# Decoder, one core: the heads' copy of causal attention placed ahead of the exponentials, its residual added by VectorE, and the opening loads split over three queues

## The reference, cut to what matters

```
L0: x1 = ln(x  + recurrence(x))                 # gates from block-diagonal w_in, w_a (8 blocks of 32x32)
    x2 = ln(x1 + retention(x1, ctx))            # position rotation and decay from tables
    x3 = ln(x2 + mixture_of_experts(x2))        # 8 experts, 2 per token
L1: x4 = ln(x3 + causal_attention(x3))          # the block that most of the change touches
    x5 = ln(x4 + cross_attention(x4, ctx))      # 16 heads
    x6 = ln(x5 + hashed_ffn(x5))
```

```
q, k, v = x3 @ wq, x3 @ wk, x3 @ wv             # per head
q, k    = rope(first half of the features), rest as it is
p       = softmax(q k^T / 128 - 1e30 * (i < j)) # i query, j key
out     = sum over heads of (p v) @ wo
x4      = ln(x3 + out)
```

## Time and profile before

| | us |
|---|---|
| median of three runs | 1661.8 (1661.14 to 1669.12) |
| the profiled execution, its own time | 1667.65 |
| its span, first to last instruction | 1665.9 |
| busy in the span: TensorE, VectorE, ScalarE, GpSimd | 1527.8, 1140.6, 801.7, 578.7 |
| mean granted clock of TensorE, as a share of full speed | 0.977 |

### The profile page before, as it was taken

How to read it: one execution, slowest core, us unless ns; L and a number is a source line. 1 busy time by engine, 2 the same in 40 slices (tenths; PEclk the granted TensorE clock), 3 DMA queues, 4 the chain that set the end, 5 groups by cost and what they waited for, 6 DMA issues and landing times.

```text
span 1665.9 us, 34482 instructions
## 1 busy us (share of the span) xinstructions
PE 1527.8 (92%) x12806; PEld 1364.2 (82%) x12806; DVE 1140.6 (68%) x2334; ACT 801.7 (48%) x1527; POOL 578.7 (35%) x679
## 2 busy tenths in 40 slices
PE   3888898899999999788888699999989999999997
PEld 2677777799999999777777578888879999999997
DVE  3899987756655565146777358877867768676775
ACT  5777742244544455236666444545434444443443
POOL 2666651212112120047776211212104444343444
PEclk8999999899999999999999899999999999999999
DMA  5122253212323330152233132121134553635443
GB/s 188 64 77 76 70 189 115 83 39 89 96 95 101 101 102 26 49 200 74 77 91 96 65 124 77 53 78 53 53 73 93 104 121 83 123 85 110 97 92 72
DMA packets 118829, 152.03 MB, mean 91 GB/s; under 512 B 10330, under 2 KB 103716, under 8 KB 118180
## 3 DMA queue, kind: packets, MB, share of 16 engines
q1 hardware_dynamic: 111540, 129.75, 28.4%
q0 software_dynamic: 6144, 16.79, 3.6%
q10 hardware_dynamic: 1008, 3.67, 0.6%
HBM read 111.37 MB, written 38.80 MB: 90 GB/s over the span
## 4 chain that ended last, share of the span: by engine, by line
PE 29%; DVE 11%; issue 7%; DMA 5%; ACT 4%; SPq 1%; POOL 1%; DVEq 0%; ACTq 0%; POOLq 0%
PE psum L518 7%; PE psum L1788 4%; DMA arena_x<-wT_d 3%; PE psum L1772 3%; PE psum L485 3%; PE psum L493 2%; PE psum L1766 2%; DVE psum L2358 2%; PE psum L1749 2%; PE psum L1488 1%; ACT arena_y L1519 1%; DMA wT_d<-arena_w 1%; DVE C_st L437 1%; PE psum L477 1%; PE psum L1485 1%
## 5 line engine op out<-in xcount | busy, mean ns | idle before, releaser
L2129 POOL TENSOR_TENSOR d_g_parts<-arena_w,d_g_parts 128x512 fp32r<-128x512 f32 x128 | 167.8, 1311 | 248.6 <-ACT d_g_parts L2261 240.9
L518 PE MATMUL psum<-d_v_high,d_g_parts 128*128 128x256 f32 x1024 | 205.1, 284 | 4.0 <-POOL d_g_parts L2129 2.3
L518 PE MATMUL psum<-d_x_parts,d_v_high 128*128 128x256 f32 x1024 | 193.5, 287 | 1.7 <-DVE d_x_parts L513 1.7
L518 PE MATMUL psum<-m_w_high,m_h_parts 128*128 128x256 f32 x1024 | 188.0, 285 | 0.0
L1192 ACT ACTIVATE arena_x<-psum,b_e 128x512 f32<-128x512 f32 x128 | 88.2, 689 | 190.1 <-PE psum L518 90.7
L518 PEld LDWEIGHTS psum<-d_v_high,d_g_parts 128*128 128x128 f32 x1024 | 167.5, 190 | 6.5 <-POOL d_g_parts L2129 4.1
L1120 POOL DMA_INDIRECT arena_x<-x_d,slot_row x64 | 66.9, 1045 | 293.6 <-PE psum L1166 229.3
L518 PEld LDWEIGHTS psum<-d_x_parts,d_v_high 128*128 128x128 f32 x1024 | 159.0, 191 | 8.6 <-DVE arena_w L2364 4.1
L518 PE MATMUL psum<-m_xF_parts,m_w_high 128*128 128x512 f32 x512 | 160.2, 395 | 2.1 <-DVE m_xF_parts L513 2.1
L518 PEld LDWEIGHTS psum<-m_w_high,m_h_parts 128*128 128x128 f32 x1024 | 160.9, 192 | 0.0
L2261 ACT ACTIVATE d_g_parts<-arena_w 128x512 fp32r<-128x512 f32 x128 | 80.8, 631 | 153.3 <-DVE arena_w L2364 152.4
(11 more groups left out here) (279 smaller groups left out, 3694.0 us busy)
## 6 DMA issues: line engine op xcount, KB each, us to landing
arena_x<-wT_d SPq DMA_DIRECT2D x128, 256.0 KB, 6.4
arena_y<-in_L_ffn_w SPq DMA_DIRECT2D x16, 1024.0 KB, 7.9
x_d<-arena_x SPq DMA_DIRECT2D x32, 256.0 KB, 2.2
y_d<-arena_x SPq DMA_DIRECT2D x16, 512.0 KB, 9.0
arena_x<-kv_d SPq DMA_DIRECT2D x16, 512.0 KB, 3.3
kv_d<-arena_x SPq DMA_DIRECT2D x9, 512.0 KB, 3.0
arena_x<-in_x SPq DMA_DIRECT2D x16, 256.0 KB, 2.9
arena_x<-in_ctx SPq DMA_DIRECT2D x16, 256.0 KB, 3.2
```

The costliest lines, as they stand in the source:

```text
L518: ins = nc.tensor.matmul(dst, left[a_], right[b_], start=start and k == 0, stop=stop and k == 2, skip_group_check=True)
L2129: nc.gpsimd.tensor_tensor(K["gP"][:, s % 4, 1], K["g"][:, s % 2], K["gP"][:, s % 4, 0].bitcast(F32), ALU.subtract).then_inc(d_gl, 1)
```

## The change

Three edits.

**1. The opening.** The first load on SP is only the identity part of the constants, then comes x of unit 0, then the six vectors and the mask. These (but for x, which has its own semaphore) count on `s_const`: N_EARLY is 8 in place of 28. Of the 16 gate blocks every second one is issued by SP and every other by ScalarE, on a semaphore of their own, `s_diag`. GpSimd issues the rest of the constants (`s_tables`) and the four weights (`s_weights`). TensorE waits for `s_diag` ahead of the first gate products and for `s_weights` in pass 4. VectorE's three instructions that read tables go into a function `setup_tables`, run in pass 2 behind a wait for the tables; GpSimd waits for the tables in its pass 2. ScalarE waits for five counts of `s_setup` in place of ten.

**2. Causal attention, residual.** The identity products are gone; the two products with `wo` start the bank. VectorE adds x3 to bank 7 into a new SBUF tile `r4` (semaphore `c_r4`), and statistics and x4 are made from `r4`. TensorE's wait for bank 7 is now for `c_r4`, and so is ScalarE's wait ahead of x3 (which four units share) and the wait in the cross attention stage.

**3. Causal attention, order.** On ScalarE the heads' copy stands ahead of the exponentials.

```diff
-        loads = [(const[:, :], a["constants"])]
+        loads, tables_in, weights_in = [], [(const[:, P:], a["constants"][:, P:])], []
...
-        N_EARLY = len(loads) + len(diag)
+        N_EARLY = 1 + len(loads)
...
         def setup_sync(sp):
+            sp.dma_start(const[:, 0:P], a["constants"][:, 0:P]).then_inc(s_const, 16)
+            sp.dma_start(A["x"][:, 0], x_u[0]).then_inc(a_in[0], 16)
             for dst, src in loads:
                 sp.dma_start(dst, src).then_inc(s_const, 16)
             sp.wait_ge(s_zero, 1)
-            for dst, src in diag:
-                sp.dma_start(dst, src).then_inc(s_const, 16)
+            for dst, src in diag[::2]:
+                sp.dma_start(dst, src).then_inc(s_diag, 16)
...
+            for dst, src in tables_in:
+                pool.dma_start(dst, src).then_inc(s_tables, 16)
+            for dst, src in weights_in:
+                pool.dma_start(dst, src).then_inc(s_weights, 16)

         def setup_scalar(act):
-
+            act.wait_ge(s_zero, 1)
+            for dst, src in diag[1::2]:
+                act.dma_start(dst, src).then_inc(s_diag, 16)
...
+        def setup_tables(dve):
+            dve.wait_ge(s_tables, 16)
+            ...                                  # even_heads, odd_heads, causal
+        N_DECAY = 5
...
+                    if t.fixed and t.n == 1:     # TensorE, ahead of the gate products
+                        pe.wait_ge(s_diag, 16 * len(diag))
...
+                if t.fixed and t.n == 2:         # VectorE
+                    setup_tables(dve)
...
                 if u3:
-                    done(pe, c_x4, u3.back(1))
+                    done(pe, c_r4, u3.back(1))
                     done(pe, c_os, u3)
                     for b in range(UB):
-                        nc.tensor.matmul(bank(7)[:, b * D:(b + 1) * D], ident, C["x3"][:, u3.c % 4, b, :],
-                                         start=True, stop=False)
                         for h in range(H1):
                             ins = nc.tensor.matmul(bank(7)[:, b * D:(b + 1) * D], C["oF"][:, h, b * S:(b + 1) * S],
-                                                   w["L1_attn_wo"][:, h, :], start=False, stop=(h == H1 - 1))
+                                                   w["L1_attn_wo"][:, h, :], start=(h == 0), stop=(h == H1 - 1))
...
+                if u3:                           # ScalarE, now ahead of the exponentials of u2
+                    done(act, c_o, u3)
+                    done(act, c_wo, u3.back(1))
+                    nc.scalar.activation(C["oF"], chunks(bank(6)), ACT.Copy).then_inc(c_os, 1)
                 if u2:
                     done(act, c_sub, u2)
...
                 if u4:                           # VectorE
                     done(dve, c_wo, u4)
-                    ln_bn(dve, u4, seqs(bank(7)), C_st4, ln4)
+                    done(dve, c_x4, u4.back(1))
+                    nc.vector.tensor_tensor(C["r4"], seqs(bank(7)), C["x3"][:, u4.c % 4], ALU.add).then_inc(c_r4, 1)
+                    done(dve, c_r4, u4)
+                    ln_bn(dve, u4, C["r4"], C_st4, ln4)
```

More of the change, by code:

```diff
@@ L283, in decoder @@
         slot_row = sb("slot_row", [P, SLOTS // P], I32)
-        s_const, s_zero = sem("s_const"), sem("s_zero")
+        s_const, s_zero, s_diag, s_tables, s_weights = (sem("s_" + n) for n in ("const", "zero", "diag", "tables", "weights"))
         s_vecT, s_vec, s_setup = sem("s_vecT"), sem("s_vec"), sem("s_setup")
@@ L307, in decoder @@
         for name in ("L0_xattn_Wq", "L0_xattn_Wk", "L0_xattn_Wv"):
[L308 to L309 removed]
+            weights_in.append((w[name][:, :, :], a[name].rearrange("(c p) n -> p c n", p=P)))
+        weights_in.append((w_route[:, :, :], a["L0_ffn_wg"].rearrange("(c p) n -> p c n", p=P)))
         loads.append((mask_in[:, :], a["mask"]))
[L311 removed]
+        N_EARLY = 1 + len(loads)
         late = []
@@ L402, in setup_vector @@
             nc.vector.tensor_scalar(mask_f[:, :], mask_in[:, :], -BIG, None, ALU.mult).then_inc(s_maskf, 1)
-            dve.wait_ge(s_maskT, 1)
-            nc.vector.tensor_copy(mask_key[:, :], bank(6)[:, 0:B]).then_inc(s_mask, 1)
             dve.wait_ge(s_vecT, 1)
@@ L408, in setup_vector @@
             nc.vector.tensor_scalar(hgate_b[:, :], vec[:, V_BIN:V_BIN + 4], 0.5, None, ALU.mult).then_inc(s_setup, 1)
+            nc.vector.tensor_scalar(ndecay[:, :], vec[:, V_A:V_A + 2], 0.0, MIN_DECAY, ALU.max,
+                                    ALU.add).then_inc(s_setup, 1)
+            dve.wait_ge(s_maskT, 1)
+            nc.vector.tensor_copy(mask_key[:, :], bank(6)[:, 0:B]).then_inc(s_mask, 1)
+            dve.wait_ge(s_act_setup, 3)
+            dve.wait_ge(s_setup, 2)
+            nc.vector.tensor_tensor(ndecay[:, :], ndecay[:, :], sp_tmp[:, 2, :], ALU.add).then_inc(s_setup, 1)
+            dve.wait_ge(s_setup, 3)
+            nc.vector.tensor_scalar(pdecay[:, :], ndecay[:, :], 0.5, None, ALU.mult).then_inc(s_setup, 1)
+            dve.wait_ge(s_setup, 4)
+            nc.vector.tensor_scalar(ndecay[:, :], ndecay[:, :], -0.5, None, ALU.mult).then_inc(s_setup, 1)
+            nc.vector.memset(mask_one[:, :], -BIG).then_inc(s_setup, 1)
+            nc.vector.tensor_copy(ident_bf[:, :], ident).then_inc(s_setup, 1)
+        def setup_tables(dve):
+            dve.wait_ge(s_tables, 16)
             nc.vector.tensor_scalar(kb_par[:, 0, :], vec[:, V_BK:V_BK + 2], table("even_heads"), None,
@@ L567, in step @@
                 u0, u3, u4, u6 = (t.at(k, UNITS) for k in (0, 3, 4, 6))
-                if u0:
+                if u0 and not (u0.fixed and u0.n == 0):
                     done(sp, aT_x, u0.back(2))
@@ L636, in step @@
                 if u4:
+                    if t.fixed and t.n == 4:
+                        pe.wait_ge(s_weights, 16 * len(weights_in))
                     done(pe, a_cF, u4)
@@ L692, in a_scalar @@
         def a_scalar(act):
-            act.wait_ge(s_setup, N_SETUP)
+            act.wait_ge(s_setup, N_DECAY)
             act.wait_ge(a_init, 2)
@@ L846, in step @@
                 if u2:
+                    if t.fixed and t.n == 2:
+                        pool.wait_ge(s_tables, 16)
                     done(pool, a_rt, u2)
@@ L1288, in decoder @@
         C["r"] = arena_y.take([P, UB, D])
+        C["r4"] = arena_y.take([P, UB, D])
         C["mx"] = arena_y.take([P, UB * H1])
@@ L1299, in decoder @@
             sem("c_" + n) for n in ("x3F", "q2", "k2", "vs", "ex", "pTs", "os"))
-        c_qt, c_qr, c_kt, c_kr, c_mx, c_sub, c_sum, c_p = (
-            sem("c_" + n) for n in ("qt", "qr", "kt", "kr", "mx", "sub", "sum", "p"))
+        c_qt, c_qr, c_kt, c_kr, c_mx, c_sub, c_sum, c_p, c_r4 = (
+            sem("c_" + n) for n in ("qt", "qr", "kt", "kr", "mx", "sub", "sum", "p", "r4"))
         ln3 = [sem("ln3_" + n) for n in ("st", "ag", "rs", "out")]
@@ L1507, in step @@
                     landed(act, c_st, u4.back(2))
-                    ln_result(act, u4, seqs(bank(7)), C["x4"][:, u4.p], C_st4, ln4)
+                    ln_result(act, u4, C["r4"], C["x4"][:, u4.p], C_st4, ln4)
                 if u1:
@@ L1522, in step @@
                     ins.then_inc(c_ex, 1)
-                if u3:
-                    done(act, c_o, u3)
-                    done(act, c_wo, u3.back(1))
-                    nc.scalar.activation(C["oF"], chunks(bank(6)), ACT.Copy).then_inc(c_os, 1)
                 if u1:
@@ L1532, in step @@
                 if u0:
-                    done(act, c_wo, u0.back(4))
+                    done(act, c_r4, u0.back(4))
                     ln_result(act, u0, C["r"], C["x3"][:, u0.c % 4], C_st3, ln3)
@@ L1796, in step @@
                 if t.fixed and t.n == 1:
-                    for part in (c_x3F, c_qr, c_kr, c_q2, c_k2, c_vs, c_x4):
+                    for part in (c_x3F, c_qr, c_kr, c_q2, c_k2, c_vs, c_r4):
                         pe.wait_ge(part, UNITS)
```

13 lines of the change are left out of this document (removed).

## The result

The changed kernel took 1649.93 us in the median of 13 runs (1646.44 to 1658.71), the kernel before 1671.29 in 13 runs beside it on the same chip. The ratio is 0.989, with an interval of 0.9869 to 0.991: 1.1% faster. Against the 1661.8 that the forecast began from that is about 18 us; the forecast of 1641.0 said 20.8, a ratio of 0.9875.

What follows compares the result with a forecast made beforehand. Issue of loads was taken to bound the opening, and a closed ring through VectorE, ScalarE and TensorE causal attention. Gains of 7.7 (opening), 9.0 (twelve passes) and 4.1 (drain) sum to 20.8: 1661.8 to 1641.0 us, range 1633 to 1652.

Steps and rivals of the forecast that it cites:

- The opening: Kernel start: fewer loads issued ahead let VectorE start earlier, 7.7 us gained, bounds 5.8 and 9.0.
- I take 7.5: Opening: VectorE's first instruction at 7.5 us in place of 15.17, between 6.2 and 9.4.
- Rival 2: Opening: small loads land only when GpSimd's queue is through, at 9.4; 5.8 gained, 1642.9 us; chance 0.14.
- The chain behind: Opening, from VectorE's start to ScalarE's first copy of x: the same 3.75 us as before.
- the tables' time in hand: Opening: tables first needed at the scan, about 20.2, landed by 9.4 at latest; over ten microseconds in hand.
- The bytes are no bound: Opening of the kernel before: DMA engines 72% busy between 8 and 9 us, 6% between 14 and 15.
- the old ring: Causal attention before: closed ring through VectorE, ScalarE and TensorE, 12.5 us; the new order was to cut it.
- ring 1: Causal attention: exponentials, ScalarE's copies, then TensorE's queries to attention products set the pass at 11.84 us; twelve gain 9.0.
- Rivals 1, 3 and 4: Causal attention: ring not cut, 1650.8 (0.14); passes of 11.58, 1637.9 (0.09); slower clock, about 1714 (0.03).
- The drain: End of causal attention: its last projections take less time, 4.1 us gained, bounds 2 and 6.
- The addition with its semaphore: Causal attention, VectorE: 0.692 for the residual addition and 0.09 for its semaphore, 0.78 us a unit.
- The next stage starts from VectorE's end of this one, so it takes all of it over: After causal attention: the drain's gain passes in full to the next stage; no loss was forecast there.

Runs made afterwards that it cites:

- e3: Changed kernel, but GpSimd issues its five loads only after the first eight small loads have landed: 1646.16 us, ratio 0.9889 to the kernel before.
- e4: Kernel before with only ScalarE's heads' copy moved ahead of the exponentials: 1660.01 us, ratio 0.9958.
- e5: Kernel before with only VectorE's residual addition in place of the identity products, heads' copy where it was: 1669.71 us, ratio 1.0021.
- e6: Changed kernel with ScalarE's copy of the values moved behind the turned-x3 copy of the next pass: 1647.73 us, ratio 0.9877 to the kernel before.
- e2: Kernel before with the edits of causal attention alone: 1651.39 us, ratio 0.992.
- e11: Changed kernel, unchanged, profiled a second time: 1647.10 us, one run.
- e9: Changed kernel with 66 idle TensorE transposes filling the waits of cross attention's opening: 1645.52 us, ratio 0.9885 to the kernel before.
- e10: Changed kernel with GpSimd's loads behind small loads and blocks, the later values' copy, and the idle-transpose filling: 1634.73 us, ratio 0.9807 to the kernel before.
- e1: Kernel before with the edits of the opening alone: 1658.90 us, ratio 0.9983.
- e7: Changed kernel with GpSimd's loads held until the small loads land and the values' copy moved later: 1646.13 us, ratio 0.9875 to the kernel before.

## Why the prediction was right and wrong

**The opening: wrong, by 3.8 us at VectorE's start.** The step that failed is "I take 7.5, nearer to the low end since the small loads alternate with the big ones instead of standing behind them". They don't alternate in any way that helps: eight small loads wait behind some 2.2 MB, and the start is 11.29. Rival 2 had the mechanism, but its 9.4 was short as well, since it took the bytes to be in by 8.7 plus 0.7 for x. That 8.7 came from a queue that began with the big table at 0.73; here GpSimd begins at 1.66 and issues its last load at 4.57, and the engines are busy until 12. The change pulled the small loads ahead on SP and, in the same edit, put the bytes on a queue that starts beside them. The chain behind (3.61 for 3.75) and the tables' time in hand (no wait) were right. The gain up to the first exponential, 3.6, is outside the stated bounds of 5.8 and 9.0. The error begins one step earlier, with "The bytes are no bound": that was read from the stretches at 8 and 14 us alone, and the same trace has the engines at 0.94 to 1.04 from 3 to 8. With issue no longer the limit, the bytes become it.

The Trainium skill's rule ("DMA: Bandwidth & Descriptors", section "Issuing engines are not separate DMA queues") says that loads of several engines run on the same 16 DMA engines and interleave. The kernel after agrees: start 11.29 with GpSimd's loads beside the small ones, 6.00 with them held back (e3).

**Causal attention: right.** The ring through ScalarE and TensorE, 11.84 forecast, is 11.82; the old ring was cut; e4 and e5 show that the order does it, and e6, by taking the values' copy out, that ring 1 was the bound. Rivals 1, 3 and 4 fell: no pass over 12.4, none at 11.58, and the granted clock is 1.00 within the passes. The drain was the term with the wide bounds: the whole stage brought 12.6 against 13.1, 9.2 of it in twelve passes (9.0 forecast) and 3.4 outside them (4.1). The addition with its semaphore was put at 0.78 and takes 0.72 (868.66 to 869.38); no run shows the 0.09 taken for the semaphore. Not said in the forecast: with the new order in place the residual's edit is worth nothing in the passes, and 1.2 us from the stage's first exponential to its end (187.8 in e2 and after, 189.0 in e4); with the old order it makes the stage 1.0 longer (e5).

**After causal attention: "The next stage starts from VectorE's end of this one, so it takes all of it over" held in one trace of the kernel after and failed in the other.** In the first it starts 16.2 us earlier, and has lost 3.5 of them by its last row maximum; in e11 it has lost nothing there. What the forecast left out is TensorE's clock in the stage's opening. It was a cost of the kernel before, too (0.67 and 0.70 granted there); how long half speed lasts differs from run to run (e11), and with the filling none of it is left in the traces (e9, e10). The Trainium skill ("TensorE: Matmul & The Clock Gate", "Part 1: The HAM clock gate") says that one kernel shows a different number of matmuls at the slow clock from run to run; the two profiles of the kernel after agree, with 7.45 and 9.58 us for the same pass. The last 3.7 us of the table are of no cause that I can show: the kernel after itself spreads there by 9.2 between its two profiles.

**Sum.** Of the 11.8 us missing between the traces, 4.1 are the opening, 0.5 causal attention, 3.5 the clock, 3.7 the last stage; the last two are within what one kernel does from run to run. The runs' ratios say the same: e2's 0.992 is 13.3 us of 1661.8 where 13.1 were forecast for causal attention, e1's 0.9983 is 2.8 where 7.7 were forecast for the opening (each known to some 5 us only). The opening is the term that was mis-sized, to less than half its size; the total came near all the same because that term is only a third of the sum.

**Open.** Why the order with the later values' copy met the longest stretch at half speed in three profiles of three, and the kernel after two lengths in two, was not settled. Whether the filling helps the kernel after itself on the chip's times was not either (e9). Nor was why the kernel before runs in two groups (about 1657 to 1667 and 1669 to 1675).

## What to carry to other kernels

When loads are moved to a second queue, add up the bytes in flight and ask which small load is waited for: a queue of its own does not let it pass, holding back the bulk until it has landed does, and then the next small load is to be looked at. In a closed ring of waits, find which engine's order closes it; moving one copy brought 11.4 us where taking work from the busiest engine brought nothing by itself. Work out a gain stage by stage, but don't book it across a stage opening in which TensorE idles: what the clock takes there can be as large as the gain, and a few microseconds of idle transposes buy it back.

## What the runs showed of the hardware

- GpSimd issues a plain DMA in 0.74 to 0.78 us, not the 1.045 of its indirect ones (after); SP issues a small vector load in 0.23 to 0.65. The issue itself grows under load: the mask's took 0.57 to 0.58 in the three profiles without GpSimd's loads beside it, and 1.29 to 1.90 in the seven with them.
- The filling of 66 transposes held the granted clock at 1.00 through 30 us (934 to 964 in e9) in which it was 0.50 to 0.91 in the kernel after.
- TensorE stayed at half speed through 10 us in which it was busy all the time (e7, 944 to 954).
- At one place of the program, where half speed is granted for a while, the same pass took 7.5, 9.6 to 9.9 or 12.7 us in twelve unfilled profiles, and nothing between; one kernel showed two of these lengths.
